# Order of the way to the first product in a fused S4D, attention and int8 kernel

## The chip, the cores and the metric

The kernel runs on one core of one Trainium2 chip. The metric is the device time of one execution in microseconds (us), the median of several.

## The reference

The reference computes one block of a model. Its first part, the token mixing, builds a kernel `K` out of decaying rotations and the input `x` (32 batches, 128 rows, 64 states, real and imaginary part):

```python
dt = jnp.exp(log_dt)
Cc = x[..., 0] + 1j * x[..., 1]
A = -jnp.exp(inv_A_real) + 1j * A_imag
dtA = A * dt[:, None]
Cc = Bc[None] * Cc * (jnp.exp(dtA) - 1.0) / A
V = jnp.exp(dtA[:, :, None] * jnp.arange(1024))
h = 2.0 * jnp.einsum('chn,hnl->chl', Cc, V).real      # (32, 128, 1024)
h = jnp.concatenate([cls_tok, h], axis=1)             # 129 rows
h = h + attention(layernorm(h), Wq, Wk, Wv, Wo)       # 32 heads, 8 key heads, causal, rope
h = h + fake_quant_ffn(layernorm(h), w, b)            # int8 per token and per channel
```

## The kernel before

There are three stages, one behind the other on every engine: mixing, attention and feed-forward. Each engine has an instruction stream of its own, written out by hand, and semaphores order them. The change lies in the mixing stage (`mix_stage`), which ends about 165 us after the start.

**Mixing.** The 1024 positions are 8 slots of 128. A power `exp(dtA * l)` is split: one table per slot (`gr`, `gi`, turned by TensorE into `g_ps`) times the powers within a slot (`eb`, for each of 128 rows). The 128 rows go in eight blocks `k` of 16, each in two halves of 8 and each half in four pairs (`PAIRS`). For each block:

- GpSimd (POOL) writes 16 phases into `yb` (L358; L373 for block 0, sixteen instructions of 128x128).
- VectorE (DVE) takes their whole part into `kb` (`whole`, L542; L605 for block 0), and the fraction is `yb` less `kb`: on GpSimd (L364), for block 0 on VectorE (L607).
- ScalarE (ACT) takes one sine over the block (L482) and 16 exponentials (`magnitudes`, L474), each with a table load when the function changes.
- VectorE multiplies them (`powers`, L537) and makes the coefficients `m1`, `m2`, which are the turned `x` (`c1`, `c2`) times the turned tables (`first_coefficients` L641 for block 0, in pairs; `coefficients` L632 for the others, in halves).
- TensorE (PE) multiplies the coefficients with `eb` (L447), ScalarE copies the result to `ho` (L512), and SyncE stores it.

On VectorE the order in block `k` is coefficients of the first half, powers, `whole(k + 1)`, coefficients of the second half.

**The start.** TensorE works through a list, `TURNS`: `x` transposed in eight turns into `c1` (`x`, L422, copied by ScalarE at L461), a small one for the rates after the third of them, then `swap` (a matmul of `c1` with a permutation, L418, copied into `c2` at L465), and `g` (four transposes of the tables in each turn, L402: two turns for the real part and two for the imaginary). Each turn waits for its input, and for its bank if that is still to be copied. There are four banks. Ahead of each half of the `g` turns stand `WARM_TURNS` matmuls on zeros (L396), whose results nothing reads. A matmul of fp32 shows as two records in the trace. VectorE makes the rates, then the fractions of block 0 (it waits for the phases from GpSimd), the slot-0 tables (`times`, L596 to L602), the magnitudes times rotations (`wj`, L613), the tables of the other slots (L596 to L602 again), and with the real part done it writes `dup` (`real_tables`, L618 and L619), with the imaginary part L625. The powers of block 0 (L537) and the first coefficients come behind them.

Of the kernel before, what the change touches and what calls it, by code (L numbers as in the profile page):

```python
# [30 lines left out]
ALU = mybir.AluOpType  # L31
# [18 lines left out]
MAGIC = 12582912.0  # L50
# [3 lines left out]
CP, CH = 16, 8  # L54
# [84 lines left out]
def at_least(eng, sem, value):  # L139

    if isinstance(value, int) and value <= 0:
        return
    eng.wait_ge(sem, value)
# [114 lines left out]
def mix_stage(nc, ctx, x, log_dt, B, inv_A, A_im, consts, h_dram, sbuf, psum, cst, ident_b, half_c, less_magic, magic,  # L258
              rows_stored, products, rows_out, powers_ready, load_next):
    OUT_BANKS = 4  # L260
    S_DECAY, S_TURN = 2 * JB, 2 * JB + 1

    def sem(name):
        return ctx.enter_context(nc.semaphore("mix_" + name))

    def block_of(slot):
        return 2 * (slot % (JB // 2)) + slot // (JB // 2)

    xin, yb, ho = sbuf["xin"], sbuf["yb"], sbuf["ho"]
    c1, c2, m1, m2 = sbuf["c1"], sbuf["c2"], sbuf["m1"], sbuf["m2"]  # L270
    dup, wj, mag, kb, sn = sbuf["dup"], sbuf["wj"], sbuf["mag"], sbuf["kb"], sbuf["sn"]
# [11 lines left out]
    swap = cst_mix[:, C_SWAP:C_SWAP + P]  # L283
# [12 lines left out]
    phases = sem("phases")  # L296
    wholes = sem("wholes")
    fracs = sem("fracs")
# [8 lines left out]
    XR = NB // 4  # L307
    PAIRS = CH // 2
    R_SMALL = 3
    WARM_TURNS = 6  # L310
    G_TURNS = 2 * JB // 4
    TURNS = [("x", i) for i in range(R_SMALL)] + [("small", 0)] + [("x", i) for i in range(R_SMALL, XR)] + \
            [("swap", i) for i in range(OUT_BANKS)] + [("g", i) for i in range(G_TURNS)] + \
            [("swap", i) for i in range(OUT_BANKS, XR)]
    COPIED = [turn for turn in TURNS if turn[0] != "g"]

    def turn_bank(r):

        return ps[(r - len(COPIED)) % OUT_BANKS]
# [62 lines left out]
    def tensor(pe, between):  # L382
# [9 lines left out]
        for kind, i in TURNS:  # L392
            if kind == "g":
                if i % (G_TURNS // 2) == 0:
                    for j in range(WARM_TURNS):
                        nc.tensor.matmul(g_ps[:, 2 * i // G_TURNS, 2 * (j % 2):2 * (j % 2) + 2, :]  # L396
                                         .rearrange("p s h -> p (s h)"), cst[:, C_ID:C_ID + P], warm[:],
                                         start=True, stop=True)
                    pe.wait_ge(turn_in, 2 + 2 * i // G_TURNS)
                for q in range(4):  # L400
                    part, slot = divmod(4 * i + q, JB)
                    mm = nc.tensor.transpose(g_ps[:, part, slot, :],  # L402
                                             dup[:, 4 * i + q].rearrange("h n r -> h (n r)"), ident)
                mm.then_inc(turned, 1)
                continue
            r = COPIED.index((kind, i))
            if kind == "x":
                pe.wait_ge(x_loaded[i], 16)
            if kind == "small":
                pe.wait_ge(turn_in, 1)  # L410
            if kind == "swap":
                pe.wait_ge(turned_out, XR + 1)
            if r >= OUT_BANKS:
                pe.wait_ge(turned_out, r - OUT_BANKS + 1)
            bank = turn_bank(r)
            if kind == "swap":
                hs = NH // XR
                mm = nc.tensor.matmul(bank[:], swap, c1[:, i * hs:(i + 1) * hs, :].rearrange("p h c -> p (h c)"),  # L418
                                      start=True, stop=True)
            elif kind == "x":  # L420
                for q in range(4):
                    mm = nc.tensor.transpose(bank[:, q * P:(q + 1) * P],  # L422
                                             xin[:, 4 * i + q].rearrange("h n r -> h (n r)"), ident)
            else:
                for q, slot in enumerate((S_DECAY, S_TURN)):
                    mm = nc.tensor.transpose(bank[:, q * P:(q + 1) * P],
                                             dup[:, slot].rearrange("h n r -> h (n r)"), ident)
            mm.then_inc(turned, 1)
# [26 lines left out]
    def scalar(act, between, load_last_rows):  # L455
        def copy_round(r):
            kind, i = COPIED[r]
            act.wait_ge(turned, TURNS.index((kind, i)) + 1)
            bank = turn_bank(r)
            if kind == "x":  # L460
                nc.scalar.copy(c1[:, :, 4 * i:4 * i + 4].rearrange("p h c -> p c h"),  # L461
                               bank[:].rearrange("p (c h) -> p c h", c=4)).then_inc(turned_out, 1)
            elif kind == "swap":
                hs = NH // XR
                nc.scalar.copy(c2[:, i * hs:(i + 1) * hs, :].rearrange("p h c -> p (h c)"),  # L465
                               bank[:]).then_inc(turned_out, 1)
            else:
                nc.scalar.copy(rates[:], bank[:, 0:2 * P].rearrange("p (q h) -> p q h", q=2)).then_inc(turned_out, 1)

        def magnitudes(k, h0, n):  # L470
            if h0 == 0:
                at_least(act, rows_ready, 2 * PAIRS * (k - 2))
            for h in range(h0, h0 + n):
                a = nc.scalar.activation(eb[:, k % 3, h, :], iota, ACT.Exp,  # L474
                                         scale=rates[:, 0, k * CP + h:k * CP + h + 1])
            if h0 + n == CP:
                a.then_inc(mags, 1)

        def sine(k):
            act.wait_ge(fracs, k + 1)  # L480
            at_least(act, powers_ready, k)
            nc.scalar.activation(sn[:], yb[:, k % 2], ACT.Sin, scale=TWO_PI_DOWN).then_inc(sin_done, 1)  # L482
# [12 lines left out]
        for r in range(R_SMALL + 1, XR + 1):  # L495
            copy_round(r)
            magnitudes(0, 2 * (r - R_SMALL - 1), 2)
        for i in range(OUT_BANKS):
            copy_round(XR + 1 + i)
        magnitudes(0, CP - 6, 6)  # L500
        sine(0)
        magnitudes(1, 0, 8)
        for i in range(OUT_BANKS, XR):
            copy_round(XR + 1 + i)
        magnitudes(1, 8, 8)
        for k in range(NCP):
            for half in range(2):
                if k >= 1:
# [14 lines left out]
    def vector(v):  # L523
# [8 lines left out]
        V = nc.vector  # L532
# [68 lines left out]
            link(V.tensor_tensor(t, ai, br, ALU.mult))  # L601
            link(V.tensor_tensor(im, im, t, ALU.add))  # L602

        v.wait_ge(phases, 1)
        V.tensor_scalar(kb[:], yb[:, 0], MAGIC, -MAGIC, ALU.add, ALU.add).then_inc(wholes, 1)  # L605
        v.wait_ge(wholes, 1)
        V.tensor_tensor(yb[:, 0], yb[:, 0], kb[:], ALU.subtract).then_inc(fracs, 1)  # L607

        v.wait_ge(b_loaded, 16)
        times(gr[:, 0, :], gi[:, 0, :], tb[:], s1[:], s2[:], bin_[:, :, 0], bin_[:, :, 1])  # L610
        v.wait_ge(sines, 3 + JB - 1)
# [2 lines left out]
        link(last)  # L614
        many = [P, JB - 1, NS]

        def real_tables():
            V.tensor_copy(dup[:, 0:JB, :, 0], gr[:])  # L618
            V.tensor_scalar(dup[:, 0:JB, :, 1], gr[:], -1.0, None, ALU.mult).then_inc(turn_in, 1)  # L619

# [30 lines left out]
        for half in range(2):  # L651
            for i in range(PAIRS):
                first_coefficients(half, i)
                if (half, i) == (0, 1):
                    whole(1)
        v.wait_ge(first_products, 2 * PAIRS)
        V.tensor_copy(ident_b[:], ident).then_inc(products, 2)
# [1 line left out]
        for k in range(1, NCP):  # L659
# [4 lines left out]
            coefficients(k, 1)  # L664

    return Engines(sync, gpsimd, tensor, scalar, vector)


# [1487 lines left out]
```

## Time and profile before

| | us |
|---|---|
| median of 3 runs | 1489.23 |
| lowest, highest | 1484.79, 1493.75 |
| profiled execution, own time | 1493.45 |
| profiled execution, span | 1491.6 |
| TensorE matmul busy | 1428.2 |
| VectorE, GpSimd, ScalarE busy | 1160.9, 921.2, 734.1 |

The span runs from the first to the last instruction in the trace. The engines work side by side, so their busy times don't add up. A wait in one of them matters only where it lies on the chain that ended last. Times in the rows are counted from the start of the span.

### The profile page before, as it was taken

The numbers are of one execution on the slowest core, as the hardware profiler recorded it, in microseconds if no ns is written. First come the engines' busy times: TensorE is split into PE (matmuls) and PEld (weight loads), VectorE is DVE, ScalarE is ACT, GpSimd is POOL, SyncE is SP. The second block draws the span as 40 slices with busy tenths as digits, with TensorE's granted clock in tenths as the row PEclk, the third lists the DMA queues.
The fourth block names the chain that finished last, engine by engine and source line by source line (L and its number), as shares of the span: only waits on it lengthen the run. The fifth ranks groups of instructions, "written<-read, shape, count | busy, mean of one in ns | idle before, by whom it ended". The sixth has DMA issues, their size and how long they took to land.

```text
span 1491.6 us, 34063 instructions
## 1 busy us (share of the span) xinstructions
PE 1428.2 (96%) x10442; PEld 1109.5 (74%) x10442; DVE 1160.9 (78%) x2285; ACT 734.1 (49%) x2673; POOL 921.2 (62%) x958
## 2 busy tenths in 40 slices
PE   5999888999999999999999999889999999999997
PEld 3999866777777777777777777676677777777774
DVE  7888678789999999999999998787765655656555
ACT  6897566576767676676767676562000000000000
POOL 5796156576767767676767767445555556455552
PEclk8999999999999999999999999999999999999998
DMA  9356666677767777777767776867434344343442
GB/s 236 102 142 152 191 142 164 181 191 204 202 200 205 201 210 194 209 194 203 200 196 206 198 206 189 259 207 200 149 113 148 116 130 134 112 145 116 133 113 60
DMA packets 264458, 255.60 MB, mean 171 GB/s; under 512 B 73329, under 2 KB 201586, under 8 KB 264402
## 3 DMA queue, kind: packets, MB, share of 16 engines
q1 hardware_dynamic: 257586, 233.87, 56.4%
q10 hardware_dynamic: 6816, 21.04, 4.7%
q8 instruction: 29, 0.48, 0.1%
q14 instruction: 27, 0.22, 0.1%
HBM read 138.26 MB, written 106.57 MB: 164 GB/s over the span
## 4 chain that ended last, share of the span: by engine, by line
PE 79%; DVE 7%; POOL 6%; DMA 3%; issue 2%; SPq 2%; ACT 1%; ACTq 0%; DVEq 0%; POOLq 0%
PE att_ps L1098 33%; PE ffn_o L1747 22%; PE ffn_y L1839 7%; PE att_ps L1141 4%; PE att_ps L1153 4%; POOL yb L358 3%; PE att_ps L1130 2%; PE att_ps L1122 2%; POOL yb L364 2%; PE mix_ps L447 1%; DMA p_blocks<-pB 1%; SPq L876 1%; PE att_ps L1109 1%; DMA xqT<-xq 1%; DVE m L641 1%
## 5 line engine op out<-in xcount | busy, mean ns | idle before, releaser
L1223 ACT ACTIVATE pr<-sm,ml 128x128 f32<-128x128 f32 x1024 | 399.1, 393 | 164.6 <-DVE ml L1401 163.3
L979 POOL TENSOR_TENSOR pr<-pr,ri 128x512 f32<-128x512 f32 x256 | 266.9, 1043 | 206.9 <-DVE ri L1408 199.8
L1098 PE MATMUL att_ps<-w_lo,xT_hi 128*128 128x512 f32 x776 | 319.9, 412 | 0.0
L1098 PE MATMUL att_ps<-w_hi,xT_hi 128*128 128x512 f32 x776 | 312.5, 403 | 3.9 <-DVE xT_lo L1349 3.1
L1098 PE MATMUL att_ps<-w_hi,xT_lo 128*128 128x512 f32 x776 | 307.6, 396 | 0.0
L1801 ACT CAST cT_hi<-ctx_in 128x512 fp32r<-128x512 f32 x64 | 36.4, 616 | 363.1 <-PE ffn_o L1747 350.8
L1747 PE MATMUL ffn_o<-wo_hi,cT_hi 128*128 128x512 f32 x528 | 211.8, 401 | 2.3 <-DVE wo_lo L1790 1.7
L1392 DVE TENSOR_TENSOR sm<-att_ps,cst 128x512 f32<-128x512 f32 x256 | 170.0, 664 | 51.9 <-PE att_ps L1141 51.9
L1747 PE MATMUL ffn_o<-wo_hi,cT_lo 128*128 128x512 f32 x528 | 205.7, 390 | 0.0
L1747 PE MATMUL ffn_o<-wo_lo,cT_hi 128*128 128x512 f32 x528 | 205.4, 389 | 0.0
L1223 ACT ACTIVATION_READ_ACCUMULATOR pr<-sm,ml 128x1 f32 x1024 | 193.4, 189 | 0.0
L1385 DVE STREAM_TRANSPOSE pB<-pr 128x512 f32<-128x512 f32 x256 | 176.3, 689 | 21.8 <-DMA p_blocks<-pB 19.6
L1401 DVE TENSOR_REDUCE ml<-sm 128x4 f32<-128x512 f32 x256 | 176.1, 688 | 9.1
L1098 PEld LDWEIGHTS att_ps<-w_hi,xT_hi 128*128 128x128 f32 x776 | 146.1, 188 | 41.2 <-issue 2.9
L1098 PEld LDWEIGHTS att_ps<-w_lo,xT_hi 128*128 128x128 f32 x776 | 146.6, 189 | 39.1 <-issue 12.5
L1098 PEld LDWEIGHTS att_ps<-w_hi,xT_lo 128*128 128x128 f32 x776 | 146.7, 189 | 28.6
L1884 DVE TENSOR_TENSOR h<-ffn_o,h_in 128x512 f32<-128x512 f32 x66 | 45.5, 690 | 148.1 <-PE ffn_o L1747 148.1
L1720 POOL TENSOR_TENSOR hb<-h,bias_sb 128x512 f32<-128x512 f32 x66 | 85.5, 1295 | 95.1 <-DVE xq L1925 60.6
L1839 PE MATMUL ffn_y<-wq,xqT 128*128 128x512 bf16 x528 | 124.9, 392 | 10.1 <-DMA xqT<-xq 10.1
L965 POOL TENSOR_SCALAR xn<-hbuf,mv,rstd 128x512 f32<-128x512 f32 x64 | 133.3, 2083 | 0.2
L1747 PEld LDWEIGHTS ffn_o<-wo_hi,cT_hi 128*128 128x128 f32 x528 | 99.2, 188 | 26.3 <-issue 3.6
L447 PE MATMUL mix_ps<-eb,m 128*128 128x128 f32 x1024 | 116.1, 275 | 1.0 <-DVE m L632 0.6
(212 smaller groups left out, 2340.7 us busy)
## 6 DMA issues: line engine op xcount, KB each, us to landing
pT<-p_blocks SPq DMA_DIRECT2D x256, 256.0 KB, 2.9
p_blocks<-pB SPq DMA_DIRECT2D x512, 64.0 KB, 2.0
h_rows<-ho SPq DMA_DIRECT2D x64, 256.0 KB, 3.8
ctx_turned<-ctxo SPq DMA_DIRECT2D x64, 256.0 KB, 3.6
h_in<-h_rows SPq DMA_DIRECT2D x32, 512.0 KB, 3.7
out_dram<-yo SPq DMA_DIRECT2D x32, 512.0 KB, 2.7
ctx_in<-ctx_turned SPq DMA_DIRECT2D x30, 512.0 KB, 3.3
hbuf<-h_rows ACTq DMA_DIRECT2D x29, 512.0 KB, 4.7
```

The source lines that it names most:

```text
L447: mm = nc.tensor.matmul(bank[:, cols], term[:, half, h, slots].rearrange("p j c -> p (j c)"), eb[:, k % 3, half * CH + h, :], start=term i ...
L965: G.tensor_scalar(xn[:, cols], hbuf[:, n[1], cols], mv[:, 0:1], rstd[:], ALU.subtract, ALU.mult).then_inc(xn_ready, 1)
L979: G.tensor_tensor(pr[:, g % 4], pr[:, g % 4], ri[:, g % 2, :].unsqueeze(2).to_broadcast([P, GQ, P]), ALU.mult).then_inc(p_ready, 1)
L1098: mm = nc.tensor.matmul(bank[:], x_part[:, t[1], e, tok:tok + P], w_part[blk][:, e, :], start=(r == 0), stop=(r == EC * 3 - 1))
L1141: mm = nc.tensor.matmul(S_BANK[j][:, q * P:(q + 1) * P], qT[rows, half, q, :], kT[rows, b[1], half, :], start=True, stop=True)
L1223: a = nc.scalar.activation(pr[:, g % 4, q, :], sm[:, g % 2, q, :], ACT.Exp, bias=ml[:, b[1], 0, h:h + 1], accum_out=ml[:, b[1], 1, h:h + 1])
L1385: V.transpose(pB[:, g % 2].rearrange("p k h f -> p h k f"), pr[:, g % 4].rearrange("p h (k f) -> p h k f", k=4)).then_inc(p_turned, 1)
L1392: V.tensor_tensor(sm[:, g % 2], S_BANK[g % 4][:].rearrange("p (q k) -> p q k", q=GQ), cst[:, C_MASK:C_MASK + P].unsqueeze(1).to_broadcast( ...
L1401: V.tensor_reduce(ml[:, b[1], 0, heads_of(g)], sm[:, g % 2], AX.X, ALU.max, negate=True).then_inc(negmax_ready, 1)
L1720: done = nc.gpsimd.tensor_tensor(hb[:, t[1], cols], h1[:, t[1], cols], bias_sb[:, cols], ALU.add)
L1747: mm = nc.tensor.matmul(O_BANK[half][:], c_part[:, t[1], e, :], w_part[:, e, half * BK:(half + 1) * BK], start=(r == 0), stop=(r == PER_HA ...
L1839: mm = nc.tensor.matmul(Y_BANK[half][:], xqT[:, c[1], e, :], wq8[:, e, half * BK:(half + 1) * BK], start=(e == 0), stop=(e == EC - 1))
```

## The change

Four orders in the mixing stage are changed.

- TensorE: all eight swap turns stand ahead of the `g` turns; before it was four ahead and four behind. `WARM_TURNS` is 4, and is used ahead of the second half of the `g` turns only; before it was 6 ahead of both halves.
- ScalarE: the last six exponentials of block 0 stand ahead of the first four swap copies instead of behind them. The first eight exponentials of block 1 stand behind the last four swap copies instead of ahead of them, with the other eight.
- VectorE: the whole parts and fractions of block 0 move behind the real tables' arithmetic and stand right ahead of `dup`.
- VectorE: the whole parts of block 1 follow the first half's fourth pair instead of its second.

```diff
-    WARM_TURNS = 6
+    WARM_TURNS = 4
     TURNS = [("x", i) for i in range(R_SMALL)] + [("small", 0)] + [("x", i) for i in range(R_SMALL, XR)] + \
-            [("swap", i) for i in range(OUT_BANKS)] + [("g", i) for i in range(G_TURNS)] + \
-            [("swap", i) for i in range(OUT_BANKS, XR)]
+            [("swap", i) for i in range(XR)] + [("g", i) for i in range(G_TURNS)]
...
-                    for j in range(WARM_TURNS):
+                    for j in range(WARM_TURNS if i > 0 else 0):
...
             copy_round(r)
             magnitudes(0, 2 * (r - R_SMALL - 1), 2)
+        magnitudes(0, CP - 6, 6)
         for i in range(OUT_BANKS):
             copy_round(XR + 1 + i)
-        magnitudes(0, CP - 6, 6)
         sine(0)
-        magnitudes(1, 0, 8)
         for i in range(OUT_BANKS, XR):
             copy_round(XR + 1 + i)
-        magnitudes(1, 8, 8)
+        magnitudes(1, 0, CP)
...
-        v.wait_ge(phases, 1)
-        V.tensor_scalar(kb[:], yb[:, 0], MAGIC, -MAGIC, ALU.add, ALU.add).then_inc(wholes, 1)
-        v.wait_ge(wholes, 1)
-        V.tensor_tensor(yb[:, 0], yb[:, 0], kb[:], ALU.subtract).then_inc(fracs, 1)
...
+        def first_fractions():
+            v.wait_ge(phases, 1)
+            V.tensor_scalar(kb[:], yb[:, 0], MAGIC, -MAGIC, ALU.add, ALU.add).then_inc(wholes, 1)
+            v.wait_ge(wholes, 1)
+            V.tensor_tensor(yb[:, 0], yb[:, 0], kb[:], ALU.subtract).then_inc(fracs, 1)
+
         def real_tables():
+            first_fractions()
             V.tensor_copy(dup[:, 0:JB, :, 0], gr[:])
...
                 first_coefficients(half, i)
-                if (half, i) == (0, 1):
+                if (half, i) == (0, PAIRS - 1):
                     whole(1)
```

## Rows read from the trace of the kernel before

**Rows 1.** Chain of waits, mixing stage: start, length (us), engine, output, line.

```profile
58.29 1.15 DVE kb L542
...
74.48 4.56 POOL yb L364
79.04 8.97 POOL yb L358 x16
...
132.75 1.23 DVE kb L542
...
138.43 16.34 PE mix_ps L447 x144
```

**Rows 2.** Timeline from 16 us: start, length, engine, line, count, idle before.

```profile
17.34 7.19 POOL L373 TENSOR_SCALAR yb<-cst_mix,rates 128x128 f32<-128x128 f32 x16 [8.60 <-ACT c L461]
...
22.87 6.37 PE L418 MATMUL mix_ps<-c,cst_mix 128*128 128x512 f32 x8 [4.86 <-ACT c L461]
...
24.50 16.46 POOL L358 TENSOR_SCALAR yb<-cst_mix,rates 128x128 f32<-128x128 f32 x16
24.64 1.23 DVE L605 TENSOR_SCALAR kb<-yb 128x2048 f32<-128x2048 f32 x1 [4.25 <-POOL yb L373]
...
24.98 0.59 ACT L465 COPY c<-mix_ps 128x512 f32<-128x512 f32 x1 [1.69 <-PE mix_ps L418]
...
25.90 2.42 DVE L607 TENSOR_TENSOR yb<-yb,kb 128x2048 f32<-128x2048 f32 x1
...
29.08 2.75 PE L396 MATMUL mix_g<-warm,cst 128*128 128x256 f32 x12
...
29.28 0.59 ACT L465 COPY c<-mix_ps 128x512 f32<-128x512 f32 x1 [0.30 <-PE mix_ps L418]
29.76 1.86 ACT L474 ACTIVATE eb<-cst_mix,rates 128x128 f32<-128x128 f32 x6
29.76 1.25 DVE L613 TENSOR_TENSOR wj<-wj,mag 128x448 f32<-128x448 f32 x2
...
31.64 1.28 ACT L482 ACT_TABLE_LOAD   x1
...
33.09 0.57 DVE L618 COPY dup<-gr 128x512 f32<-128x512 f32 x1
...
34.04 1.09 PE L402 MATMUL mix_g<-cst,dup 128*128 128x128 f32 x8 [2.21 <-DVE dup L619]
...
34.97 4.44 PE L396 MATMUL mix_g<-warm,cst 128*128 128x256 f32 x12
...
35.97 0.90 DVE L625 TENSOR_SCALAR dup<-gi 128x512 f32<-128x512 f32 x2
...
40.12 3.60 PE L418 MATMUL mix_ps<-c,cst_mix 128*128 128x512 f32 x8
40.32 2.48 DVE L641 TENSOR_TENSOR m<-c,mix_g 128x512 f32<-128x512 f32 x4 [1.25 <-PE mix_g L402]
```

**Rows 3.** The same timeline from 42 us.

```profile
43.56 14.45 PE L447 MATMUL mix_ps<-eb,m 128*128 128x128 f32 x128
...
48.56 6.96 POOL L358 TENSOR_SCALAR yb<-cst_mix,rates 128x128 f32<-128x128 f32 x16
...
51.62 4.47 DVE L632 TENSOR_TENSOR m<-c,mix_g 128x2048 f32<-128x2048 f32 x2
51.77 1.91 ACT L482 ACTIVATE sn<-yb 128x2048 f32<-128x2048 f32 x1
```

**Rows 4.** Timeline of GpSimd at 70 us, one phase of block 3.

```profile
70.11 2.60 POOL L358 TENSOR_SCALAR yb<-cst_mix,rates 128x128 f32<-128x128 f32 x1
```

**Rows 5.** Stretches: length, busy PE, PEld, DVE, ACT, POOL, granted clock, DMA, GB/s.

```profile
26.00:28.00 2.00, 2.00 (x3) 0.67 (x2) 2.00 (x1) 0.59 (x1) 2.00 (x2) 0.50 1.02 209
28.00:29.00 1.00, 1.00 (x3) 0.45 (x2) 0.97 (x4) 0.59 (x1) 1.00 (x2) 0.86 1.06 250
```

**Rows 6.** Stretch of GpSimd's phases (L358): length, busy (count), granted clock, DMA.

```profile
29.70:36.20 6.50, 6.50 (x7) 0.92 1.04 219
```

## Prediction

> **What bounds the kernel now.** I read the profile from the outside in. The table above gives a span of 1491.6 us, and the profiled execution took 1493.45 us, so 1.85 us lie around the span, and this execution is 4.2 us above the median of the runs, 1489.23. The change touches only the mixing stage at the start, so the question is how much of its first 165 us sets the end.
>
> Next the chain of waits over the mixing stage [rows 1]. From 58.29 on it repeats one pattern: VectorE's `kb` (L542, 1.24), GpSimd's subtraction (L364, 4.56), GpSimd's 16 phases of the next block (L358, about 9.0), `kb` again. The first of these `kb` starts at 58.29 and the last at 132.75, which is five periods of 14.89 us. Only then does TensorE's run of products at 138.43 take over, and the attention stage follows. So what the start can give to the end is what it gives to the `kb` at 58.2, the one of block 2. The chain goes from the phases to `kb`, so VectorE was waiting for them each time; TensorE and ScalarE aren't in the pattern.
>
> Then the timeline of the start [rows 2]. GpSimd makes the phases of block 0 from 17.34 to 24.53. VectorE sits idle for them (4.25 us before the `kb` at 24.64), takes the fractions until 28.32, and only then makes the tables, though these need nothing of the phases. TensorE does four swap turns at half clock from 22.87, and twelve records of warm-up, waits, turns the real tables at 34.04, runs twelve more warm-up records until 39.41, turns the imaginary ones, and after these the other four swaps from 40.12 to 43.72. VectorE's first coefficients start at 40.32. After that VectorE is the bound: sixteen coefficient operations of 0.62, `kb` 1.24 and some 0.4 of `ident_b` are 11.5 us, and the coefficients of block 1 start 11.3 after 40.32 [rows 2, 3]. Two of 2.2 and powers of 2.2 bring it to the `kb` at 58.2.
>
> **The change, part by part.**
>
> *Tables ahead of fractions.* The six small products (from the fractions' end at 28.32 to 29.76, taken as 1.5) and the two of `wj` (1.25) move to 20.4, where VectorE's block ends now (24.64 less the 4.25 of idle). Behind them come the three real-table products, from 31.01 to 33.09, 2.08. They end at 20.4 + 1.5 + 1.25 + 2.08 = 25.25. Their inputs are there: at 24.64 VectorE waits for the phases alone, and the sines, the magnitudes and B had come before 20.4. Now VectorE stands in GpSimd's way. Eleven table operations run during the phases of block 0. A free phase takes 0.45 (7.19 for 16 [rows 2]); under the larger table operations seven took 6.5, 0.93 each [rows 6]. From 21.9 to 25.25 that is some four phases in place of seven, so I end block 0 at 26.2 in place of 24.53. The fractions then run 26.3 to 30.0 (1.23 + 2.42 and gaps). Bounds: 24.6 if the operations did no harm, which gives 28.3 as now, and 27.0 if all table operations, the small ones too, held phases to 0.93 each (five until 25.25, and the four left at 0.45).
>
> *Real and imaginary tables.* `dup` of the real part starts at 30.0 in place of 33.09: 3.1 us sooner, ready at 30.9. The imaginary one is ready at 36.87 - 3.1 = 33.8. The powers need the sine of block 0. ScalarE has copied the first four swaps at 29.87 (six exponentials no longer stand in between, they fill its wait of 1.69 ahead of the first copy), then table load 1.28 and sine 1.91 [rows 2, 3]: 29.9 or 30.0 + 3.2 = 33.2. So powers run from 33.8 to 36.0. The last four swap copies and the 16 exponentials of block 1 follow on ScalarE: 33.2 + 4 x 0.59 + 1.28 + 16 x 0.306 = 41.7.
>
> *Swaps ahead of tables, eight warm-up turns fewer (12 become 4).* Up to 29.2 TensorE does the same as before. The granted clock is 0.50 until 28 and 0.86 in the microsecond after it [rows 5], so it rose at 28.3; the fourth swap ends at 29.2 in both. Swaps five to eight at full clock are 3.6 us as at 40.12, hence 32.8. Their banks are free: the first copy is out at 25.6. Real tables 1.09: 33.9. Four warm-up turns are eight records of 0.23 (12 took 2.75 at full clock): 35.7. Imaginary tables: ready since 33.8, 1.0: 36.7. TensorE has no wait in all this, where it now has one of 2.2 us, after which the clock fell and twelve records took 4.44.
>
> So the first coefficients start at 36.75 in place of 40.32: 3.6 us sooner. TensorE starts its products one pair (1.24) later, at 38.0 in place of 43.56, 5.5 sooner, as no swaps stand ahead of them now.
>
> *The whole of block 1 after four pairs in place of two.* Block 1's phases on GpSimd begin at 26.2 and are held by the fractions (two phases, until 30.2), then four get through until 33.8, one is held by the powers until 36.0, and nine at 0.45 end at 40.1. VectorE reaches `kb` after eight operations of 0.62: 36.75 + 4.95 = 41.7. It doesn't wait. Before it stood at 42.72. So this handshake comes only 1.0 us sooner: 2.5 of the 3.6 are given to the two pairs. GpSimd subtracts from 42.95 to 47.5 and starts the phases of block 2 there (48.56 now).
>
> *The handshake of block 2, where it is decided.* VectorE does the same work in another order, so all of it comes 3.6 sooner: coefficients at 51.62 - 3.6 = 48.05 to 52.45, powers to 54.65. TensorE's first half of block 0 is done at 38.0 + 7.2 = 45.2, so the coefficients don't wait; sine 1 is done at 47.5 + 3.2 = 50.7 at the latest. VectorE could take `kb` at 54.65. But the phases now run into the powers. Today those of block 2 run from 48.56 to 55.5 (6.96) and powers start at 56.0, just after. Later blocks show the clash: 16 phases take 8.97 [rows 1], 2.0 more than 6.96, and it is in one instruction, of 2.60 at 70.11 [rows 4], when the powers ran. From 47.5 eleven phases are through at 52.45, the twelfth is held until 54.9, four more take 1.8: 56.7. So `kb` of block 2 comes at 56.7 in place of 58.2, and of 3.6 us only 1.5 are left. From there each period is 14.9 as before, since it always held one clash. The end moves by -1.5 us, hidden by nothing: the products at 138.43 follow on that chain.
>
> The Trainium skill, SBUF - State Buffer, Who interferes with whom, says that a VectorE instruction with two SBUF inputs and a GpSimd one that reads SBUF block each other, whoever comes first. It speaks against this change: with the rule the sum is the -1.5 above, without it -3.6. The trace agrees in the 2.60 of that phase.
>
> Bounds of the sum: 0 if something holds GpSimd for 1.5 us more (the phases of block 1 late at 41.7, or a second operation that holds those of block 2), -3.6 if nothing does.
>
> **The rivals.**
>
> *A, as above:* against the profiled execution 1493.45 - 1.5 = 1491.9; against the median 1489.23 - 1.5 = 1487.7.
>
> *B, all of VectorE's lead carries:* 1489.2 - 3.6 = 1485.6. It needs phases of block 2 that aren't held. Against it stands the 2.60 phase; the later blocks all show its 9.0 for 16 phases.
>
> *C, the start is absorbed, so the change doesn't do what it says:* GpSimd's phases of block 0 or 1 are held longer, or the attention stage, which waits for transfers of its own, swallows 1.5 us. Time 1489.2. For it: the first part's bound alone lies 0.8 us to the bad side, half of the gain. Against it: at 41.7 there are 1.6 us of room before the phases of block 1 would be late.
>
> *D, slower: the clock doesn't rise.* The eight swaps and the first turns all stand ahead of the tables now, and the twelve warm-up records that came at 29.08 are gone. If the clock rose only after them, eight swaps would end at 22.87 + 8 x 1.72 = 36.6 (between the first and the fourth copy, 24.98 and 29.28, lie two swaps at half clock and one at full: 4.30 = 5 x 0.86), real tables 2.2, warm-up 8 x 0.42 = 3.4 (twice 2.75 / 12, a little less for its tail), imaginary 2.1: 44.3. The coefficients would start 4.0 later, `kb` of block 1 at 49.3, 6.6 us later than now, and the chain with it: 1495.8. Each microsecond at half clock costs half of one, so the kernel gets slower than before from a rise later than 28.3 + 2 x 1.5 = 31.3. Against it: the clock rose at 28.3 while only swaps had run. The Trainium skill, TensorE: Matmul & The Clock Gate, Part 1: The HAM clock gate, says that TensorE's own activity releases the clock, and that the point varies between runs; by the first half D is out and by the second a small part of it stays. The trace agrees with the first, in the rise at 28.3.
>
> **How the numbers follow.** A 0.60, B 0.13, C 0.21, D 0.03, something of several us that I don't see 0.03. Predicted 1487.7. What can be told from no change is 0.5%, 7.4 us; the three runs of before lie 9 us apart, from 1484.8 to 1493.75. No case but D comes near 7.4, so the chances come from the scatter: a median at 1487.7 is faster by over 7.4 with 0.07, slower with 0.04, within it 0.89. The range takes B (1485.6) and C (1489.2), each widened by some 3 us for the scatter of a median: 1482.8 to 1492.3.
>
> **What would show it right or wrong** in the changed kernel: VectorE's tables from 20.4 with no gap, first `kb` at 26.3 (24.6 to 27.0); TensorE without a wait from 22.9 to 36.7 and a granted clock of 1.00 from 29 on; first coefficients at 36.75; first products of TensorE at 38.0; `kb` of block 1 at 41.7 with no wait for phases; a phase of some 2.5 us in block 2 and its `kb` at 56.7 behind a wait of 2 us; the last one at 131.3; the products now at 138.43 at 137.0. The prediction is wrong if `kb` of block 2 comes at 54.7 (B) or at 58 (C), if swaps five to eight take 1.7 each (D), or if the last `kb` moved and the end of the mixing stage didn't.

## The result, and the profile after

Beside the kernel before, the changed kernel took 1485.88 us (14 runs, 1480.18 to 1488.08) against 1489.55 (14 runs, 1484.79 to 1494.75): ratio 0.9968, 95% interval 0.9954 to 0.9982, so 2.7 to 6.9 us faster, 4.8 by the ratio itself. (The two medians alone lie 3.7 us apart, 0.9975; all ratios here are those on record, another estimate from the same single times.) A second measurement, below, gives 0.9952, 7.2 us. That the change makes the kernel faster is clear. By the first interval it is less than 0.5%; the second, 0.9935 to 0.9970, leaves that open. The forecast was 1487.7 us, in the range 1482.8 to 1492.3. The sign is as forecast; by this interval the size is two to five times the 1.5 us of the sum.

The timeline of the changed kernel from 16 us (start, length, engine, line, tile, count, idle before), beside [rows 2, 3]:

```profile
17.51 9.30 POOL L372 TENSOR_SCALAR yb<-cst_mix,rates 128x128 f32<-128x128 f32 x16 [8.86 <-ACT c L460]
...
23.06 9.61 PE L417 MATMUL mix_ps<-c,cst_mix 128*128 128x512 f32 x16 [4.69 <-ACT c L460]
...
26.92 1.40 DVE L612 TENSOR_SCALAR kb<-yb 128x2048 f32<-128x2048 f32 x1 [1.71 <-POOL yb L372]
...
28.36 2.41 DVE L614 TENSOR_TENSOR yb<-yb,kb 128x2048 f32<-128x2048 f32 x1
...
31.18 1.91 ACT L481 ACTIVATE sn<-yb 128x2048 f32<-128x2048 f32 x1
...
32.52 1.04 PE L401 MATMUL mix_g<-cst,dup 128*128 128x128 f32 x8
...
33.39 1.89 PE L395 MATMUL mix_g<-warm,cst 128*128 128x256 f32 x8
34.16 2.28 DVE L535 TENSOR_TENSOR eb<-eb,sn 128x2048 f32<-128x2048 f32 x1
...
35.12 1.04 PE L401 MATMUL mix_g<-cst,dup 128*128 128x128 f32 x8
...
36.37 4.86 DVE L641 TENSOR_TENSOR m<-c,mix_g 128x512 f32<-128x512 f32 x8
...
41.15 1.22 DVE L540 TENSOR_SCALAR kb<-yb 128x2048 f32<-128x2048 f32 x1
...
42.45 4.56 POOL L363 TENSOR_TENSOR yb<-yb,kb 128x2048 f32<-128x2048 f32 x1 [1.56 <-DVE kb L540]
...
46.97 9.01 POOL L357 TENSOR_SCALAR yb<-cst_mix,rates 128x128 f32<-128x128 f32 x16
...
51.83 2.28 DVE L535 TENSOR_TENSOR eb<-eb,sn 128x2048 f32<-128x2048 f32 x1
...
56.02 1.23 DVE L540 TENSOR_SCALAR kb<-yb 128x2048 f32<-128x2048 f32 x1 [1.91 <-POOL yb L357]
```

TensorE has one row of matmuls behind the other from 23.06 to 36.16, where it had a wait of 2.21 and a slow row of warm-up [rows 2]. Its granted clock is 0.50 until 28, 0.96 in the next microsecond and 1.00 from 29 on. The first coefficients start at 36.37 in place of 40.32. The `kb` of block 1 doesn't wait, and that of block 2 does: powers run at 51.83 inside the phases at 46.97, these take 9.01 in place of 6.96 [rows 3], and `kb` comes at 56.02 in place of 58.2. One phase of the sixteen holds nearly all of the difference. It starts just before the powers:

```profile
51.69 2.58 POOL L357 TENSOR_SCALAR yb<-cst_mix,rates 128x128 f32<-128x128 f32 x1
```

The chain of waits at the end of the mixing stage, beside [rows 1]:

```profile
130.28 1.23 DVE kb L540
...
135.95 16.34 PE mix_ps L446 x144
```

The product run that the chain ends in starts 2.48 us sooner. That is the mixing stage's part. But the spans of the two profiled executions lie 6.2 us apart (1491.6 and 1485.4), and between the start of the product run and the first load of the attention stage's loop, 149.8 us have become 146.2. The row of that load (start of the first and the last of 26, before and then after) shows it:

```profile
L838 ACTq MOVE hbuf<-h_rows x26: 29/29/29, 288.2 to 891.5; - x26
```

```profile
L838 ACTq MOVE hbuf<-h_rows x26: 29/29/29, 282.1 to 885.2; - x26
```

Nothing of the diff lies there. So the experiments have two questions: is the mixing stage's part what the sum says, and where do the other microseconds come from?

### The profile page after: what moved, and what is told of

It reads as the page before. It is cut to its first block, busy times and chain, and to the rows that moved or that the text cites. A ratio compares the mean times of both kernels' runs of the same rounds, so it can differ in the third digit from the quotient of the medians.

```text
span 1485.4 us, 34032 instructions
## 1 busy us (share of the span) xinstructions
PE 1421.9 (96%) x10426; PEld 1106.7 (75%) x10426; DVE 1160.7 (78%) x2285; ACT 733.1 (49%) x2673; POOL 921.5 (62%) x958
## 4 chain that ended last, share of the span: by engine, by line
PE 81%; POOL 7%; DVE 5%; DMA 3%; issue 2%; ACT 1%; SPq 1%; ACTq 0%; DVEq 0%; POOLq 0%
PE att_ps L1098 35%; PE ffn_o L1747 22%; PE ffn_y L1839 7%; PE att_ps L1141 5%; PE att_ps L1153 4%; POOL yb L357 4%; PE att_ps L1130 2%; POOL yb L363 2%; PE att_ps L1122 2%; PE mix_ps L446 1%; PE att_ps L1109 1%; DMA p_blocks<-pB 1%; DMA xqT<-xq 1%; POOL yb L372 1%; DVE kb L540 1%
## 5 line engine op out<-in xcount | busy, mean ns | idle before, releaser
L1747 PE MATMUL ffn_o<-wo_hi,cT_hi 128*128 128x512 f32 x528 | 211.8, 401 | 2.0 <-ACT wo_hi L1785 1.4
L1747 PE MATMUL ffn_o<-wo_hi,cT_lo 128*128 128x512 f32 x528 | 205.7, 390 | 0.0
L1747 PE MATMUL ffn_o<-wo_lo,cT_hi 128*128 128x512 f32 x528 | 205.4, 389 | 0.0
L1098 PEld LDWEIGHTS att_ps<-w_hi,xT_hi 128*128 128x128 f32 x776 | 146.5, 189 | 41.2 <-issue 2.7
L446 PEld LDWEIGHTS mix_ps<-eb,m 128*128 128x128 f32 x1024 | 116.7, 194 | 5.1 <-DVE eb L535 2.1
```

Of the source, the lines that this page charges most:

```text
L446: mm = nc.tensor.matmul(bank[:, cols], term[:, half, h, slots].rearrange("p j c -> p (j c)"), eb[:, k % 3, half * CH + h, :], start=term i ...
L1098: mm = nc.tensor.matmul(bank[:], x_part[:, t[1], e, tok:tok + P], w_part[blk][:, e, :], start=(r == 0), stop=(r == EC * 3 - 1))
L1747: mm = nc.tensor.matmul(O_BANK[half][:], c_part[:, t[1], e, :], w_part[:, e, half * BK:(half + 1) * BK], start=(r == 0), stop=(r == PER_HA ...
```

## The experiments

All ratios are to the kernel before on the same chip, with 95% intervals, as are the intervals on which differences rest; one such interval is 2 to 3 us to either side.

**1. The kernel before again.** No edit.

> The kernel before, unchanged, to see how far two executions of one kernel lie apart and in which stage. Theory 1 (the change gives its gain in the mixing stage alone, about 2.5 us, and what the two profiles show beyond that is scatter of later stages): the kb of block 2 again at 58.2 +- 0.2 us, the last kb at 132.7 +- 0.3, the start of the last product run at 138.4, while the first projection matmul (174.5 in the first profile) and the last feed-forward matmul (1470.3) vary by 1 to 4 us. Theory 2 (the attention stage itself answers to the earlier start with another 1 us or more): the later marks agree with the first profile within 0.5 us too, so that the 6.2 us between the spans are real. Ratio to before 1.000 +- 0.0015 by both.

Measured: 1.0006 (0.9990 to 1.0021). `kb` of block 2 at 58.09, the last at 132.49, product run at 138.16: the mixing stage repeats within 0.3 us. The later marks don't: the last feed-forward matmul (L1747, first of its three products) is at 1474.1, 3.5 us later than the 1470.6 of the first profile. A difference of a few us between two single profiles behind the mixing stage can be scatter.

**2. The changed kernel again.** No edit.

> The changed kernel, unchanged, beside the others of this call. Ratio 0.9968 +- 0.0015 by the measurement at hand; by theory 1 (2.5 us of mixing stage and nothing else) 0.9983. Last kb at 130.3, start of the last product run at 135.9; last feed-forward matmul anywhere from 1464 to 1468 by theory 1, at 1464.8 +- 0.5 by theory 2 (attention stage gains too).

Measured: 0.9952 (0.9935 to 0.9970). Last `kb` at 130.06, product run at 135.73, last feed-forward matmul at 1462.5. The two measurements put the gain at 4.8 and 7.2 us, and theory 1's 0.9983 lies outside both intervals, though only just outside the first (0.9982). The loop's first load comes 145.7 us behind the product run; in the two profiles of before it is 149.8 and 148.9.

**3. Whole parts of block 1 back after the second pair.**

```diff
-                if (half, i) == (0, PAIRS - 1):
+                if (half, i) == (0, 1):
                     whole(1)
```

> The changed kernel with the whole parts of block 1 back after the second pair. Phases of block 1 ended at 40.9 there; VectorE would reach this kb after four operations at 38.8 and wait until 40.9 for it. Theory A (GpSimd's chain decides from block 1 on): kb of block 1 ends at 42.1 in place of 42.4, the subtraction starts 0.25 us sooner, the phases of block 2 are held by powers that come 1.9 us later, and kb of block 2 is at 55.8 to 56.0, as in the changed kernel; the second half's coefficients lose 2 us that nobody waits for. Theory B (what counts is VectorE's lead, and the move after the fourth pair is what gave the gain): kb of block 2 at 58.0 as in the kernel before, and the time of the kernel before. Ratio 0.997 (A), 1.000 (B).

Measured: 0.9980 (0.9964 to 0.9996). The timeline of VectorE:

```profile
40.78 1.23 DVE L540 TENSOR_SCALAR kb<-yb 128x2048 f32<-128x2048 f32 x1 [2.09 <-POOL yb L357]
56.25 1.21 DVE L540 TENSOR_SCALAR kb<-yb 128x2048 f32<-128x2048 f32 x1
```

`kb` of block 1 now waits 2.09 us for its phases, and starts only 0.37 sooner. `kb` of block 2 is at 56.25, 0.23 later than in the changed kernel, since VectorE is what it waits for. Product run at 136.21. Theory A holds: the move after the fourth pair is worth 0.26 us against the first profile of the changed kernel and 0.48 against the second, which is little more than two profiles of one kernel differ by.

**4. The `kb` of block 2 three times, all else as changed.**

```diff
-            V.tensor_scalar(kb[:], yb[:, k % 2], MAGIC, -MAGIC, ALU.add, ALU.add).then_inc(wholes, 1)
+            for n in range(times_over):
+                t = V.tensor_scalar(kb[:], yb[:, k % 2], MAGIC, -MAGIC, ALU.add, ALU.add)
+                if n + 1 < times_over:
+                    link(t)
+            t.then_inc(wholes, 1)
...
-                whole(k + 1)
+                whole(k + 1, 3 if k == 1 else 1)
```

> The changed kernel with the kb instruction of block 2 run three times in place of once, so that only this handshake comes 2.5 us later and all of the start stays as changed. Theory 1 (the gain is the place of kb of block 2, passed on one to one): last kb at 132.8, the product run at 138.4, ratio 1.0017 of the changed kernel, all but the time of before. Theory 2 (the earlier first products, rows and loads give part of the gain by another way): last kb at 132.8 too, but the time stays 1.2 us or more under the kernel before. Theory 3 (the mixing stage after block 2 isn't bound by this chain, so the delay is swallowed): last kb under 131.5.

Measured: 0.9975 (0.9959 to 0.9990). The first row is VectorE's timeline, the second the chain of waits:

```profile
56.10 3.75 DVE L541 TENSOR_SCALAR kb<-yb 128x2048 f32<-128x2048 f32 x3 [1.91 <-POOL yb L357]
```

```profile
138.37 11.65 PE mix_ps L446 x102
```

A delay of 2.5 us at this handshake is still 2.4 to 2.6 us at the product run (138.37 against 135.95 and 135.73): the chain passes it on one to one. But the kernel stays faster than before by 3.7 us (1.5 to 6.1 by the interval), with its product run where it was in the kernel before. So some gain doesn't come through the chain, as theory 2 says of the time; by which other way isn't shown here. The kernels so far with such a gain share the earlier start, which theory 2 names, but also a shorter program of TensorE: eight warm-up matmuls less are 32 records, since each is two matmuls and two weight loads. The next runs part the two.

**5. The kernel before with a shorter TensorE program.** The twelve startup matmuls on zeros go; nobody reads their results.

```diff
-        for j in range(4):
-            nc.tensor.matmul(ps[0][32 * j:32 * j + 32, 0:2 * PB], warm[:, 0:32], warm[:], start=True, stop=True)
-        for i in range(2):
-            for j in range(4):
-                nc.tensor.matmul(ps[j][:, i * PB:(i + 1) * PB], warm_r[32 * j:32 * j + 32, 0:P],
-                                 warm_r[32 * j:32 * j + 32, 0:PB], start=True, stop=True)
```

> The kernel before without its twelve startup matmuls on zeros (1.35 to 3.05 us), so that TensorE's program is shorter by as much as the changed kernel's is (8 fp32 matmuls are 32 records; these twelve are 32 too), while nothing of the order from 7 us on is touched. Question: the changed kernel gains about 3 us behind the mixing stage, with the last product run at the same place (late_whole2). Theory P (place: what lies behind in TensorE's program is fetched at other moments since the program is shorter): last product run at 138.4 as before, ratio 0.998, first load of the attention loop 146 us behind the last product run (149 in the kernel before). Theory M (moment: the attention stage answers to when the start's work was done, not to the program's length): ratio 1.000 +- 0.0015, loop 149 us behind. If the clock starts low without these matmuls, transposes at 7 to 13 us take longer, which ScalarE's copies (one per 1.4 us) hide.

Measured: 0.9985 (0.9967 to 1.0003). Product run at 138.12, as before; the loop's first load 148.1 us behind it. The ratio is nearer to theory P's, but the interval holds 1, and the 148.1 is nearer to the 149 of theory M than to the 146 of theory P. Inconclusive alone.

**6. The changed kernel with a longer TensorE program.** The same startup matmuls twice (`for again in range(2):` around them).

> The changed kernel with its twelve startup matmuls twice, so that TensorE's program is as long as before, all in the idle time ahead of 7 us. Theory P: last kb at 130.3 and product run at 135.9 as in the changed kernel, but the loop 149 us behind it as before; ratio 0.9984 (the mixing stage's 2.4 us alone). Theory M: loop 146 us behind, ratio 0.996 to 0.997.

Measured: 0.9981 (0.9963 to 0.9999). The chain of waits and the row of the loop's loads:

```profile
135.84 14.22 PE mix_ps L447 x125
```

```profile
L839 ACTq MOVE hbuf<-h_rows x26: 29/29/29, 285.2 to 887.7; - x26
```

The product run is where the changed kernel has it, the loop's first load 149.4 us behind it, as in the kernel before. What is left, 2.8 us, is the mixing stage's 2.4. Twelve matmuls on zeros at 1 to 5 us, while TensorE waits for its first input, take away 2 to 4 us of the gain by the ratios themselves, all of it behind 136 us. This is as theory P said, but the ratio's interval still holds the 0.9968 of the changed kernel's first measurement, so the time alone doesn't exclude theory M.

**7. VectorE's tables ahead of the fractions, alone.** The diff's part in `vector`, but for `whole(1)`.

> The kernel before with VectorE's tables ahead of the fractions alone; TensorE's and ScalarE's order, the warm-up turns and whole(1) after the second pair as before. By the sum on record: tables 2.5 us sooner (30.7), imaginary ones ready at 34.3, first half of the tables turned, twelve warm-up records at full clock 2.8 us, second half at 36.5, coefficients from 37.0 (3.4 sooner), but four swaps behind the tables keep TensorE from products until 40.3, and c2 of later pairs has no wait. Phases of block 1 end at 40.9, so kb of block 1 waits and ends at 42.1; kb of block 2 at 56.0 to 56.6. Ratio 0.9985 in the mixing stage alone, 0.997 if the attention stage gives as much as in the changed kernel.

Measured: 0.9981 (0.9962 to 0.9999). VectorE waits for the sine before the powers (35.49), which I had not counted; first coefficients at 37.78, `kb` of block 2 at 56.26. Then something else than expected. GpSimd's timeline, blocks 2 and 3 and later:

```profile
46.63 6.90 POOL L358 TENSOR_SCALAR yb<-cst_mix,rates 128x128 f32<-128x128 f32 x16
...
62.09 6.89 POOL L358 TENSOR_SCALAR yb<-cst_mix,rates 128x128 f32<-128x128 f32 x16
...
77.91 9.02 POOL L358 TENSOR_SCALAR yb<-cst_mix,rates 128x128 f32<-128x128 f32 x16
```

For two blocks the powers fall behind the phases and hold none (6.9); VectorE and TensorE are the bound there, since the swaps behind the tables let the products start at 39.96 only. From block 4 on they clash again (9.02). The product run starts at 137.22: of 1.95 us at block 2, 1.1 to 1.2 are left. The loop's first load is 146.2 us behind it, which is what the shorter programs have, though this one is as long as before.

**8. TensorE's and ScalarE's part alone.** `TURNS`, the warm-up turns and ScalarE's order as changed, `vector` as before.

> The kernel before with TensorE's swaps ahead of the tables, four warm-up turns in place of twelve, and ScalarE's order; VectorE as before. Real tables ready at 34.0 as now, turned until 35.1; TensorE has 1.3 us of wait ahead of them; four turns 1.9 to 3.0, imaginary tables ready at 36.9, turned until 38.1; powers until 39.1; coefficients at 39.1 (1.2 sooner), kb of block 1 at 41.6, kb of block 2 at 57.0, each 1.1 sooner. Theory P: 0.9972 (1.1 us and 3 us behind). Theory M: 0.999.

Measured: 0.9975 (0.9956 to 0.9994). `kb` of block 1 at 41.15, of block 2 at 56.61, product run at 136.58: 1.6 to 1.8 us sooner, more than the 1.1 expected. The loop's first load is 146.0 behind it.

**9. The changed kernel with twelve warm-up turns.** `WARM_TURNS = 6`, ahead of both halves.

> The changed kernel with the twelve warm-up turns of before (six ahead of each half of the table turns). They stand where TensorE has no wait now: six more turns ahead of the real tables, 1.4 to 2.8 us, and two more ahead of the imaginary ones, 0.5. First coefficients 1.9 to 3.3 us later than 36.4, so kb of block 1 at 43.0 to 44.5 and kb of block 2 at 57.9 to 59. Theory P (TensorE's program is as long as before, and this costs 2.3 us behind the mixing stage): time of the kernel before or 1 us above, ratio 1.000 to 1.001. Theory M (only the moments count): ratio 0.998 to 0.999, 3 us behind the start given back by the kb and the rest of the gain kept.

Measured: 1.0015 (0.9996 to 1.0035). `kb` of block 2 at 58.91, product run at 138.86. Twelve turns in place of four undo the whole change: 3.0 us come through the chain and the rest behind it. That rest doesn't lie where theory P has it: the loop's first load is 146.5 us behind the product run, as with the shorter programs. TensorE's timeline:

```profile
32.13 2.75 PE L395 MATMUL mix_g<-warm,cst 128*128 128x256 f32 x12
34.72 1.04 PE L401 MATMUL mix_g<-cst,dup 128*128 128x128 f32 x8
35.59 2.75 PE L395 MATMUL mix_g<-warm,cst 128*128 128x256 f32 x12
38.19 1.04 PE L401 MATMUL mix_g<-cst,dup 128*128 128x128 f32 x8
```

**10. The kernel before with four warm-up turns, nothing moved.** `WARM_TURNS = 4`, none ahead of the real tables.

> The kernel before with four warm-up turns in place of twelve (none ahead of the real tables) and nothing moved. TensorE waits from 29.2 to 34.0, so its clock may be low in the table turns: real tables until 36.2, four turns until 38.1 to 40, imaginary tables 1 to 2 us: coefficients from 39.2 to 41.8 (40.3 in before), kb of block 2 within 1.5 us of 58.2. Theory P: ratio 0.9975 to 0.9985, since the program is 32 records shorter, as in before_short. Theory M: ratio 1.000, or the move of kb of block 2 alone.

Measured: 0.9976 (0.9959 to 0.9992). TensorE now waits 4.55 us ahead of the real tables and is at half clock in them:

```profile
33.87 1.97 PE L402 MATMUL mix_g<-cst,dup 128*128 128x128 f32 x8 [4.55 <-DVE dup L619]
35.64 3.48 PE L396 MATMUL mix_g<-warm,cst 128*128 128x256 f32 x8
```

Yet `kb` of block 2 is at 57.77 and the product run at 138.03, a little ahead of before. So the mixing stage gains 0.3 us, no more than it varies by, and the kernel 3.6 (1.2 to 6.1). The loop's first load is 145.2 us behind the product run. By the ratios themselves two lines of the diff give half of its time or more, and neither an earlier start nor a moved order is needed for that.

**11. The changed kernel without warm-up turns.**

```diff
-                    for j in range(WARM_TURNS if i > 0 else 0):
+                    for j in range(0):
```

> The changed kernel without any warm-up turn. TensorE turns the imaginary tables when they are ready: 34.25 + 1.0 in place of 36.16, then the powers end at 36.4 and are no bound for coefficients; these start at 35.4 to 36.5, behind the powers on VectorE, so at 36.5 as now. Nothing in the mixing stage moves: kb of block 2 at 56.0, last kb at 130.3. The program is 16 records shorter than the changed kernel's. Theory P says that the time may move by up to 3 us either way with that; theory M says 0.996 to 0.997, as the changed kernel.

Measured: 0.9972 (0.9955 to 0.9989). `kb` of block 2 at 56.14, product run at 136.28, the loop's first load 146.3 behind it. The last four turns buy nothing that can be measured, and cost nothing.

**12. The handshake of `kb` in two halves of 8 rows.** An attempt to take GpSimd's wait out of the chain.

```diff
         def fraction(k):
-            pool.wait_ge(wholes, k + 1)
-            nc.gpsimd.tensor_tensor(yb[:, k % 2], yb[:, k % 2], kb[:], ALU.subtract).then_inc(fracs, 1)
+            for a in range(2):
+                hs = slice(a * CH, (a + 1) * CH)
+                pool.wait_ge(wholes, 2 * k + a)
+                t = nc.gpsimd.tensor_tensor(yb[:, k % 2, hs], yb[:, k % 2, hs], kb[:, hs], ALU.subtract)
+            t.then_inc(fracs, 1)
...
-                whole(k + 1)
+                whole(k + 1, 0)
+                whole(k + 1, 1)
```

> The changed kernel with the handshake of kb in two halves of 8 rows for blocks 1 to 7, so that VectorE has the whole parts of the first half done while GpSimd still makes the second half's phases. If the chain of kb, subtraction and phases is the bound of the mixing stage, its period of 14.87 us loses 1.34 (GpSimd's wait for kb) or, if VectorE's second kb has to wait until GpSimd's first subtraction is done (both use SBUF, 2.3 us), only 0.6. TensorE needs 14.45 us for a block, so the period ends at 14.45 or 14.3 to 14.5: five periods give 1.5 to 2.1 us, last kb at 128.2 to 128.8, and the product run at 133.9 to 134.4. Ratio 0.995. If the chain isn't the bound, the last kb stays at 130.3.

Measured: 0.9988 (0.9971 to 1.0005), a smaller gain than the changed kernel's, where 0.995 was expected. The timelines of VectorE and of GpSimd in block 3:

```profile
70.23 0.68 DVE L546 TENSOR_SCALAR kb<-yb 128x1024 f32<-128x1024 f32 x1
71.18 2.83 DVE L546 TENSOR_SCALAR kb<-yb 128x1024 f32<-128x1024 f32 x1 [0.27 <-POOL yb L357]
```

```profile
71.12 2.35 POOL L367 TENSOR_TENSOR yb<-yb,kb 128x1024 f32<-128x1024 f32 x1
74.10 2.38 POOL L367 TENSOR_TENSOR yb<-yb,kb 128x1024 f32<-128x1024 f32 x1 [0.63 <-DVE kb L546]
76.45 9.54 POOL L357 TENSOR_SCALAR yb<-cst_mix,rates 128x128 f32<-128x128 f32 x16
```

The second `kb` takes 2.83 in place of 0.68: it stands until GpSimd's first subtraction is done. GpSimd saves 0.7 of its wait and loses it in the phases (9.54: the held one takes 3.10 in place of 2.58, from 82.89 until just after the first `kb` is done) and in the split subtraction, so the period is 14.84, unchanged. VectorE is 1.9 us later with the coefficients (73.94 against 72.04), and the product run starts at 137.82. The loop's first load is 150.0 behind it, the most of all profiles, with the shorter program. The Trainium skill, SBUF - State Buffer, Who interferes with whom, says that a `tensor_scalar` on VectorE can hold the port pair which it shares with GpSimd, and that the one that comes second stands still. This run shows it in the direction in which GpSimd came first.

## Why the prediction was right, and where it fell short

The mixing stage, step by step as on record:

| step | forecast | measured |
|---|---|---|
| phases of block 0 end | 26.2 | 26.8 |
| fractions end | 30.0 | 30.8 |
| swaps end; TensorE's waits | 32.8; none | 32.7; none |
| first coefficients | 36.75 | 36.37 |
| first products on TensorE | 38.0 | 37.74 |
| `kb` of block 1, wait | 41.7, none | 41.15, none |
| `kb` of block 2, wait | 56.7, 2 us | 56.02, 1.91 |
| last `kb` | 131.3 | 130.28 |
| product run | 137.0 | 135.95 |

- **Tables ahead of fractions.** Right in kind. GpSimd's phases were held a little more (9.30 for 16, 8.9 forecast), so the fractions came 0.8 late. It didn't matter: `dup` was ready at 31.45, and TensorE was in the swaps until 32.67.
- **Swaps ahead of tables.** Right. The clock rose while the swaps ran, so rival D is out. What came last before the first coefficients was not the step forecast, though: TensorE's turn of the imaginary tables ended at 36.16, not 36.7, and the coefficients followed VectorE's own powers (34.16 to 36.44). Run 10 shows that a low clock in the real tables costs nothing even without the swaps ahead: the coefficients there start at 40.03.
- **Two more pairs ahead of `kb` of block 1.** Right that it costs no wait. Run 3 against the two profiles of the changed kernel puts its worth at 0.2 to 0.5 us.
- **The clash at block 2.** Right, and it is what keeps rival B out: VectorE was ready at 54.1 and waited 1.91, with one phase of 2.58 as forecast. B's time, 1485.6, lies next to the measured 1485.88, but its mechanism isn't what happened: the rest of the gain came from behind the mixing stage, so the nearness is luck.
- **The term mis-sized.** The move of `kb` of block 2, forecast 1.5, is 2.2. GpSimd's subtraction of block 1 started 0.5 sooner than forecast, and phases with a clash took 9.01 where the count of single ones gave 9.2. Another 0.3 comes in the later blocks, whose period is 14.85 in place of 14.91, so the product run moved by 2.4 to 2.6. Alone, VectorE's part gave 1.1 of this (run 7) and TensorE's and ScalarE's part 1.7 (run 8).
- **The step that failed: "The end moves by -1.5 us".** It took for granted that all behind the mixing stage moves with it. The chain itself does so (run 4), but the kernel gained another 2.3 and 4.7 us behind it in its two measurements. That the time still fell into the range is in part luck, since the range was widened for scatter and not for this. The table puts the runs beside each other: where the product run starts against before (138.3, mean of its two profiles), the measured ratio as us of 1490, the remainder, and how far the loop's first load lies behind the product run in the profile (149.8 in the first one of before).

| kernel | TensorE's program | product run | measured | remainder | first load behind the product run |
|---|---|---|---|---|---|
| before again | as before | -0.1 | +0.9 | +1.0 | 148.9 |
| changed, startup twice | as before | -2.5 | -2.8 | -0.3 | 149.4 |
| tables alone | as before | -1.1 | -2.8 | -1.7 | 146.2 |
| changed, 12 turns | as before | +0.6 | +2.2 | +1.6 | 146.5 |
| before, no startup | 32 records less | -0.2 | -2.2 | -2.0 | 148.1 |
| before, 4 turns | 32 less | -0.3 | -3.6 | -3.3 | 145.2 |
| turns alone | 32 less | -1.7 | -3.7 | -2.0 | 146.0 |
| `kb` three times | 32 less | +0.1 | -3.7 | -3.8 | 145.9 |
| second pair | 32 less | -2.1 | -3.0 | -0.9 | 145.5 |
| changed (two measurements) | 32 less | -2.5 | -4.8, -7.2 | -2.3, -4.7 | 146.2, 145.7 |
| halves | 32 less | -0.5 | -1.8 | -1.3 | 150.0 |
| changed, no turns | 48 less | -2.0 | -4.2 | -2.2 | 146.3 |

A single remainder has about 2.5 us of uncertainty, and one of the long programs (-1.7) lies among those of the short. But the mean of the four long ones is 0.2 and that of the eight values with 32 records less is -2.5, a difference of 2.7 with some 1.8 to either side if the twelve are taken as independent, and the pairs that differ in the startup matmuls alone (runs 5 and 6) go the same way. The last column is less clear: tables alone and run 9 are long with 146.2 and 146.5, runs 5 and 12 are short with 148.1 and 150.0. So it is likely, but not shown beyond doubt, that the length of TensorE's program ahead of the attention stage is worth some 2.5 us behind the mixing stage. Why it would be so is open. The profile lists transfers of the kind "instruction", and their number is the same in all fourteen profiles (29 packets on one queue, 27 on another); no wait of an engine is put down to them, and none of the runs tests them. What the profile shows is where TensorE sits without a cause that it names. In the attention loop (290 to 880 us) TensorE's waits put down to "issue" ahead of its transposes (L1130) come to 3.2 to 5.1 us in the five profiles with the long program and 1.3 to 3.6 in the eight with 32 records less; the two groups overlap. The granted clock differs as well. Stretches of TensorE (length, busy, count, granted clock, DMA, GB/s), before and then after:

```profile
138.00:175.00 37.00, 33.41 (x276) 0.95 0.53 132
...
250.00:270.00 20.00, 17.97 (x131) 0.91 0.67 185
270.00:290.00 20.00, 17.73 (x160) 0.91 0.60 161
```

```profile
138.00:175.00 37.00, 32.87 (x278) 1.00 0.61 156
...
250.00:270.00 20.00, 18.63 (x170) 1.00 0.71 200
270.00:290.00 20.00, 18.78 (x168) 1.00 0.73 207
```

The clock is at its lower level for 10.2 us between 140 and 288 in the kernel before, and for 3.4 in the changed one; the other profiles have 0 to 13.7. Where it is 3.4 or less, the loop's first load comes 145.2 to 146.3 us behind the product run, and where it is over 13, 148.9 to 150.0; in between (6.8 to 10.2) it is anything from 145.9 to 149.8. The first fall, the 0.95 above, can be followed. Sixteen transposes of TensorE behind the same wait, before and then after:

```profile
168.41 3.51 PE L1065 MATMUL att_ps<-cst,raw 128*128 128x128 f32 x16 [1.04 <-DVE xT_lo L1315]
```

```profile
165.94 1.94 PE L1065 MATMUL att_ps<-cst,raw 128*128 128x128 f32 x16 [1.05 <-DVE xT_lo L1315]
```

All fourteen profiles have this wait and one of 1.58 us ahead of it. The clock falls about them in six: in three of the five with the long program (both profiles of before, run 6) and in three with the short (runs 4, 5 and 12). So neither the waits nor the length of the program alone decides whether it falls.

The clock of a whole execution is on record for nearly every single run. Its mean is 0.9853 for the kernel before and 0.9884 for the changed one in the second measurement. Among executions of one kernel, 0.001 more clock goes with 0.76 us less time (a fit over the kernels of this record). By this, an estimate, 2.4 of the 7.2 us go with the clock. So a part of the gain goes with a TensorE that is at half clock less often. Whether the length of the program makes that, or both follow from something else, none of the runs separates: tables alone has the long program and 3.4 us, and its mean clock, 0.9877, is above that of most of the short ones.

The forecast of "within 0.5%" rested on the mixing stage and on scatter. The first measurement bears it out (4.8 us, at most 6.9); with 7.2 in the other the kernel sits near the edge of that bound of 7.4.

## What to carry to other kernels

Follow the handshake that the rest of a stage is paced by, and price an earlier start only at that place: here 3.9 us of lead at the first coefficients became 2.2 at `kb` of block 2, and 2.5 arrived at the stage's end. When a change adds or takes away instructions, even dummies, test that alone: a version with the same order and another program length tells a gain of the new order from one that isn't in it. Warm-up matmuls need a run without them: here twelve of them in place of four, where TensorE no longer waits, cost as much as the whole change gave or more.

## What the runs showed of the hardware

- TensorE's program shorter by 32 records near its start went, on the mean of the runs, with 2.7 us less behind the mixing stage (8 values against 4; runs 5, 6 and 10 with nothing else moved). Single profiles don't all follow it, and the cause is open.
- The same waits of TensorE, 1.58 and 1.04 us, went together with a fall of the granted clock in six profiles and with none in eight; 16 transposes took 3.51 us with it (before) and 1.94 without (changed).
- A `tensor_scalar` of VectorE over 128x1024 fp32 took 2.83 us in place of 0.68 when a two-input subtraction of GpSimd had begun 0.06 us ahead of it.
- VectorE's operations that read one input from PSUM (L632) ran beside GpSimd's phases without any harm: 16 phases took 6.9 us beside them, and 9.0 only with powers in between, when a single phase took 2.58 in place of 0.45.
